# A relation layer in which POOL waits for free gather buffers once a step instead of once a unit

## The chip, the cores and the metric

The kernel runs on one core of a Trainium2 chip. The metric is the device time of one execution in microseconds (us). Engines are named as the profile names them: PE (TensorE matmul) and PEld (its weight loads), DVE (VectorE), ACT (ScalarE), POOL (GpSimd), SP (SyncE, which here only issues DMAs). "L796" is line 796 of the kernel.

## What is computed

A graph of N = 6250 nodes with 128 features and E = 200000 edges, sorted by destination. Two residual blocks, each followed by a layer norm: a two-layer weighted-mean aggregation, and then the relation layer that the change touches. Cut to that layer:

```python
# x1: the first block's result (6250, 128); 32 relations, 8 bases
hsrc = h[src]                                   # one row of x1 per edge
coef = w_comp[etype]                            # (E, 8)
msg = sum(hsrc @ weight[b] * coef[:, b][:, None] for b in range(8)) * norm
node_repr = segment_sum(msg, dst, num_segments=N) + bias_param
x = layernorm(x1 + relu(node_repr))
```

## The kernel before

The edges stand in 1568 tiles of 128. The first 428 tiles (REGION) are treated without gathers: their edges were sorted by source, and their source rows are made on PE by a product with a one-hot matrix (`sources`, L1283; ACT copies the result, L994; PE turns it, L1318; ACT copies that, L1001; "wide" products with it, L1326, which DVE adds up, L1777). The other 1140 tiles are gathered: POOL fetches one row of x1 for each of the 128 edges of a tile with an indirect DMA (L796).

The stage runs in 114 steps. A step has ten gathered tiles (STEP_TILES) in two units of five (UNIT_TILES), "tile 0" and "tile 1" of the step. A unit's five tiles are multiplied by PE (`tiles_summed`, L1309: ten matmul records, since each product is two in the trace) and the result is added into a ring of sums by DVE (`tile_added`, L1768). The gathered rows lie in G, which has room for HELD_UNITS = 7 units: unit n, where n = 2 x step + half, uses place n mod 7.

Each engine works through an order written out by hand, and semaphores tie them together. The counter s_u counts the units that PE has finished, in PE's order (`UNIT` gives a unit's number in it, with the wide and turned ones). s_gath[place] counts what has landed in a place; PE waits for it ahead of a unit's product (`tiles_summed`). The order of PE in a step s is: tile 0 of s (L1309), a part of the sources for step s+2 (L1283), two wide products (L1326), more sources, the finished blocks of nodes ("events", `block_multiplied`, L1345, which ACT takes in `block_taken`, L1020), two wide products, tile 1 of s (L1309), the last sources, the coefficients of s+2 (L1265, L1269), the turned sources of s+1 (L1318). Then tile 0 of s+1 follows. So tile 1 of a step and tile 0 of the next stand close together, and between tile 0 and tile 1 of one step lies most of its work. About every second step has an event.

DVE makes the one-hot matrices (L1718 to L1748), loads ring positions into registers (L1752) and adds. SP issues plain DMAs for the next steps.

POOL's program in this stage is only the loop that the change touches. Ahead of the first tile of each unit from the eighth on, it waits until PE has finished the unit that lies in the same place, seven units earlier. In the trace the wait is carried by the gather itself.

Of the kernel before, what the change touches and what calls it, by code (L numbers as in the profile page):

```python
# [38 lines left out]
HELD_UNITS = 7  # L39
# [195 lines left out]
def regular(nc, flag, x, src, dst, etype, w, w1, lin1, b1, lin2, b2, Wrel, wcomp, brel, out):  # L235
    with ExitStack() as ctx:
# [449 lines left out]
        def _(pool):  # L686
# [103 lines left out]
            for t in range(REGION, TILES):  # L790
                step, j = divmod(t - REGION, STEP_TILES)
                n, i = 2 * step + j // UNIT_TILES, j % UNIT_TILES
                if i == 0 and n >= HELD_UNITS:
                    half = n - HELD_UNITS
                    pool.wait_ge(s_u, UNIT[half // 2, "tile", half % 2] + 1)
                pool.indirect_dma_start(G[:, n % HELD_UNITS * UNIT_TILES + i, :], None, x1_d,  # L796
                                        bass.IndirectOffsetOnAxis(ap=SRC[:, t:t + 1], axis=0)).then_inc(s_gath[n % HELD_UNITS], 16)
# [2236 lines left out]
```

## Time and profile before

| | us |
|---|---|
| time, median of 3 runs (lowest to highest) | 3873.58 (3860.37 to 3875.08) |
| the profiled execution's own time | 3908.11 |
| its span, first to last instruction | 3906.3 |

The page's first two parts:

```profile
PE 3433.9 (88%) x17077; PEld 2289.0 (59%) x17077; DVE 2464.7 (63%) x4684; ACT 1351.4 (35%) x3452; POOL 2412.9 (62%) x2636
```

```profile
PE   3999999989989999999996888888888888888895
POOL 5888888870036675454523666666666666666662
PEclk6999999999999999999998888888888889888887
```

The first line is busy time, share of the span and number of instructions of each engine. In the strips the span is cut in 40 slices of 97.7 us, and a digit is the busy share in tenths; PEclk is the granted TensorE clock. The relation layer is the last 18 slices, from about 2100 us on. There PE is busy eight tenths of the time and POOL six, at a steady pace, and the clock is granted at 0.8 to 0.9.

### The profile page before, as it was taken

What the parts mean: (1) busy time and instruction counts of PE and PEld (TensorE: products, weight loads), DVE (VectorE), ACT (ScalarE), POOL (GpSimd) and SP (SyncE); (2) the same over time, 40 slices, a digit from 0 to 9 for tenths busy, and PEclk for the clock granted to TensorE, in tenths of its full rate; (3) what the DMA queues carried; (4) which work ended last, traced back from release to release, by engine and by line L of the source; (5) the groups of instructions that cost most, each with busy time, mean ns of one, the idle gap of its engine ahead of it and who ended that gap; (6) DMA issues with size and microseconds to landing.
All of it is one profiled execution on the core that took longest, in us unless ns stands there. A gap on an engine that the chain in (4) does not pass through costs nothing.

```text
span 3906.3 us, 52705 instructions
## 1 busy us (share of the span) xinstructions
PE 3433.9 (88%) x17077; PEld 2289.0 (59%) x17077; DVE 2464.7 (63%) x4684; ACT 1351.4 (35%) x3452; POOL 2412.9 (62%) x2636
## 2 busy tenths in 40 slices
PE   3999999989989999999996888888888888888895
PEld 3899999985533334444343555666555565555664
DVE  7999999986776663021032665666666666666674
ACT  5999999990000000010002222222222222222221
POOL 5888888870036675454523666666666666666662
PEclk6999999999999999999998888888888889888887
DMA  6677777778789999999993222222222222222221
GB/s 184 193 206 205 205 209 208 206 208 297 259 236 248 254 242 261 288 273 277 288 294 105 63 65 70 65 73 61 69 70 65 70 68 73 71 65 65 71 63 41
DMA packets 532789, 618.45 MB, mean 158 GB/s; under 512 B 74011, under 2 KB 460127, under 8 KB 532399
## 3 DMA queue, kind: packets, MB, share of 16 engines
q1 hardware_dynamic: 478895, 528.52, 47.3%
q0 software_dynamic: 53616, 86.51, 8.9%
q8 instruction: 140, 2.29, 0.2%
q14 instruction: 138, 1.13, 0.1%
HBM read 445.83 MB, written 168.99 MB: 157 GB/s over the span
## 4 chain that ended last, share of the span: by engine, by line
PE 47%; ACT 19%; DMA 9%; DVE 8%; issue 8%; another core or an unknown queue 7%; DVEq 2%; POOL 1%; SPq 0%; ACTq 0%; POOLq 0%
PE PS L1230 20%; ACT arena L844 11%; PE PS L1283 10%; DMA arena<-adjacency 8%; ACT arena L860 6%; PE PS L1309 5%; PE PS L1326 4%; PE PS L1269 2%; PE PS L1118 2%; DVE XT L1768 2%; PE PS L1345 1%; PE PS L1318 1%; DVEq L1752 1%; DVE H L1748 1%
## 5 line engine op out<-in xcount | busy, mean ns | idle before, releaser
L796 POOL DMA_INDIRECT arena<-x_table,rec x1140 | 1165.2, 1022 | 602.5 <-issue 311.0
L775 POOL DMA_INDIRECT sorted_records<-arena x428 | 494.2, 1155 | 590.4 <-PE PS L1230 495.3
L1118 PE MATMUL PS<-arena 128*98 128x128 f32 x6272 | 761.8, 279 | 46.6 <-DVE arena L1507 13.0
L1118 PEld LDWEIGHTS PS<-arena 128*98 128x98 f32 x6272 | 708.5, 166 | 96.4 <-issue 50.8
L732 POOL TENSOR_SCALAR arena<-iota,H,arena 128x98 f32<-128x98 f32 x980 | 677.5, 705 | 89.2 <-PE PS L1118 86.6
L1283 PE MATMUL PS<-H,X 128*128 128x512 bf16 x1568 | 549.3, 436 | 80.9 <-issue 76.4
L1230 PE MATMUL PS<-arena,X 128*128 128x512 f32 (+1 forms) x1274 | 543.8, 578 | 53.8 <-DMA arena<-adjacency 53.6
L844 ACT ACTIVATE arena<-arena 128x98 f32<-128x98 f32 x1568 | 583.4, 688 | 12.7 <-DVE arena L1505 12.7
L1230 PE MATMUL PS<-arena,H 128*128 128x512 f32 (+1 forms) x1274 | 531.9, 572 | 18.7 <-DMA arena<-adjacency 16.9
L1768 DVE TENSOR_TENSOR XT<-XT,PS 128x64 f32 x1140 | 252.5, 221 | 432.3 <-issue 198.4
L860 ACT ACTIVATE arena<-PS 98x1024 f32<-98x1024 f32 x392 | 520.5, 1328 | 12.6 <-PE PS L1118 12.6
L1686 DVE TENSOR_TENSOR arena<-arena 128x1536 f32<-128x1536 f32 (+1 forms) x192 | 344.1, 1792 | 174.0 <-DMA arena<-adjacency 168.1
L1507 DVE TENSOR_TENSOR arena<-PS,H 128x2048 f32<-128x2048 f32 x196 | 447.1, 2281 | 0.0
L1230 PEld LDWEIGHTS PS<-arena,X 128*128 128x128 f32 x1274 | 237.3, 192 | 339.1 <-issue 196.4
L1230 PEld LDWEIGHTS PS<-arena,H 128*128 128x128 f32 x1274 | 238.0, 190 | 300.8 <-issue 213.2
L1309 PE MATMUL PS<-arena 128*128 128x64 f32 x2280 | 325.3, 293 | 57.2 <-issue 45.8
L1309 PEld LDWEIGHTS PS<-arena 128*128 128x128 f32 x2280 | 323.0, 214 | 89.7 <-issue 55.8
L1283 PE MATMUL PS<-H,arena 128*128 128x512 bf16 x784 | 338.7, 432 | 6.2 <-issue 5.8
L1326 PE MATMUL PS<-arena 128*128 128x336 f32 x896 | 313.9, 474 | 27.9 <-issue 18.2
L1777 DVE TENSOR_TENSOR arena<-arena,PS 128x336 f32 x448 | 224.8, 502 | 178.1 <-remote 95.7
L1283 PEld LDWEIGHTS PS<-H,X 128*128 128x128 bf16 x1568 | 171.9, 116 | 266.2 <-issue 174.6
L994 ACT ACTIVATE rec<-PS 128x512 f32<-128x512 f32 x112 | 66.7, 596 | 677.7 <-remote 423.9
(259 smaller groups left out, 3148.0 us busy)
## 6 DMA issues: line engine op xcount, KB each, us to landing
arena<-adjacency SPq DMA_DIRECT2D x294, 768.0 KB
adjacency<-arena SPq DMA_DIRECT2D x196, 784.0 KB
arena<-adjacency SPq DMA_DIRECT2D x98, 832.0 KB
arena<-x_table,rec POOLq DMA_INDIRECT x1140
XT<-sorted_source_rows SPq DMA_DIRECT2D x112, 128.0 KB
arena<-in_edge_type SPq DMA_DIRECT2D x226, 48.0 KB
arena<-in_edge_type SPq DMA_DIRECT2D x226, 32.0 KB
XT<-sorted_relations SPq DMA_DIRECT2D x448, 8.0 KB
```

Source lines behind the costliest of these rows:

```text
L732: last = nc.gpsimd.tensor_scalar(S1[:, r, :], iota[:, 0:M1], K1T[:, v:v + 1], WWT[:, v:v + 1], ALU.is_equal, ALU.mult)
L775: pool.indirect_dma_start(rec2_d, bass.IndirectOffsetOnAxis(ap=SLOT[:, t:t + 1], axis=0), R4[:, t, :], None).then_inc(s_scat, 16)
L796: pool.indirect_dma_start(G[:, n % HELD_UNITS * UNIT_TILES + i, :], None, x1_d, bass.IndirectOffsetOnAxis(ap=SRC[:, t:t + 1], axis=0)).the ...
L844: nc.scalar.activation(S1[:, r, :], S1[:, r, :], ACT.Copy, scale=WWT[:, v:v + 1]).then_inc(s_wa, 1)
L860: nc.scalar.activation(ST[0:M1, n % 3, q * GROUP * P:(q + 1) * GROUP * P], PS[0:M1, q * GROUP * P:(q + 1) * GROUP * P], ACT.Copy).then_inc ...
L1118: last = nc.tensor.matmul(bank(2 * q + j // 4, P, j % 4 * P)[0:M1, :], S1[:, r, :], S2[:, r, :], start=True, stop=True)
L1230: last = nc.tensor.matmul(bank(bank0 + c, nb * P), (X, H1)[l][:, k, :], AB[n % 4][:, off:off + nb * P], start=(k == 0), stop=(k == NBLK - 1))
L1283: last = nc.tensor.matmul(bank(2), rows_part, ST2[i % 2][:, j, :], start=(j == 0 and a == 0), stop=(j == CLASS_BLOCKS - 1 and a == 2))
L1309: last = nc.tensor.matmul(bank(UNIT_BANKS[n % RING_BANKS], BASIS, j * BASIS), G[:, half % HELD_UNITS * UNIT_TILES + j, :], C[s % 2][:, fir ...
L1326: nc.tensor.matmul(bank(UNIT_BANKS[n % RING_BANKS], WIDE_BASIS), G2[i % 2][:, c, :], C2[i % 2][:, c, :, :].rearrange("p b j -> p (b j)"), ...
L1507: nc.vector.tensor_tensor(S2[:, whole, :], bank(4, P).unsqueeze(1).to_broadcast([P, BATCH, P]), each(K2T, n).to_broadcast([P, BATCH, P]), ...
L1686: nc.vector.tensor_tensor(ACC[p % 2][:, 0:width], ACC[p % 2][:, 0:width], AB[n % 4][:, 0:width], ALU.add).then_inc(s_acc, 1)
```

## The change

The one condition ahead of the gathers changes. Before, POOL waited at the first tile of each unit n (i == 0) for unit n - 7. After, it waits only at the first tile of a step (j == 0, n even), and for unit n + 1 - 7 = n - 6, the one whose place the second unit of this step will take. s_u counts in order, so unit n - 7 is then done as well. The ten gathers of a step follow without a further wait. The first wait comes at unit 6 instead of unit 7.

```diff
             for t in range(REGION, TILES):
                 step, j = divmod(t - REGION, STEP_TILES)
                 n, i = 2 * step + j // UNIT_TILES, j % UNIT_TILES
-                if i == 0 and n >= HELD_UNITS:
-                    half = n - HELD_UNITS
+                if j == 0 and n + 1 >= HELD_UNITS:
+                    half = n + 1 - HELD_UNITS
                     pool.wait_ge(s_u, UNIT[half // 2, "tile", half % 2] + 1)
                 pool.indirect_dma_start(G[:, n % HELD_UNITS * UNIT_TILES + i, :], None, x1_d,
```

## Rows read from the trace of the kernel before

**Rows 1.** The gathers' source line: count, ns min/median/max, who waited for it.

```profile
L796 POOL DMA_INDIRECT arena<-x_table,rec x1140: 941/947/2315, 2103.6 to 3848.2; - x190
...
who waited for it (us, times):
```

**Rows 2.** Timeline of PE, end of the stage: start, us, instruction.

```profile
3876.47 1.23 PE L1309 MATMUL PS<-arena 128*128 128x64 f32 x10
```

**Rows 3.** Windows view, whole stage: busy us of PE, PEld, DVE, ACT, POOL; clock, DMA.

```profile
2165.00:3848.20 1683.20, 1452.07 (x7461) 993.21 (x7458) 1084.99 (x3222) 438.07 (x1086) 1121.51 (x1097) 0.86 0.27 68
```

**Rows 4.** Waits of POOL, 2165 to 3850 us: us in total, times, longest.

```profile
POOL arena L796 <- issue: 298.8, 978, 0.7
POOL arena L796 <- PE PS L1309: 127.3, 47, 9.9
POOL arena L796 <- remote: 110.2, 55, 2.8
```

**Rows 5.** Timeline of POOL, first gathers of bursts, with idle before in brackets.

```profile
2151.92 0.94 POOL L796 DMA_INDIRECT arena<-x_table,rec  x1 [3.46 <-remote]
...
3083.08 1.46 POOL L796 DMA_INDIRECT arena<-x_table,rec  x1 [1.93 <-PE PS L1309]
...
3112.78 0.96 POOL L796 DMA_INDIRECT arena<-x_table,rec  x1 [2.27 <-PE PS L1309]
...
3143.02 1.10 POOL L796 DMA_INDIRECT arena<-x_table,rec  x1 [2.01 <-PE PS L1309]
...
3203.41 0.94 POOL L796 DMA_INDIRECT arena<-x_table,rec  x1 [2.19 <-remote]
3218.06 0.95 POOL L796 DMA_INDIRECT arena<-x_table,rec  x1 [2.15 <-remote]
```

**Rows 6.** Timeline of PE, 3068 to 3220 us: unit products and one event.

```profile
3112.18 0.30 PE L1309 MATMUL PS<-arena 128*128 128x64 f32 x1 [0.51 <-issue]
...
3115.54 1.23 PE L1309 MATMUL PS<-arena 128*128 128x64 f32 x10
...
3141.53 1.22 PE L1309 MATMUL PS<-arena 128*128 128x64 f32 x10
...
3145.38 1.23 PE L1309 MATMUL PS<-arena 128*128 128x64 f32 x10
...
3195.59 1.95 PE L1345 MATMUL PS<-XT,Wr 128*128 128x128 f32 x16
```

**Rows 7.** Timeline of ACT, the event's copy.

```profile
3202.98 0.37 ACT L1020 ACTIVATE H<-PS,bcol 128x128 f32<-128x128 f32 x1 [11.64 <-remote]
```

**Rows 8.** Windows view, sums: first 8 us of nine bursts; then rest up to next.

```profile
sum 72.00, PE 70.86 PEld 46.73 DVE 41.74 ACT 32.51 POOL 56.63; mean PE 7.87 PEld 5.19 DVE 4.64 ACT 3.61 POOL 6.29
...
sum 63.00, PE 45.93 PEld 33.39 DVE 44.39 ACT 2.42 POOL 35.38; mean PE 5.10 PEld 3.71 DVE 4.93 ACT 0.27 POOL 3.93
```

**Rows 9.** Windows view of PE, eight steps: length, PE busy, clock, DMA.

```profile
3082.30:3095.80 13.50, 12.18 (x61) 0.87 0.32 69
3095.80:3116.80 21.00, 16.16 (x82) 0.84 0.24 60
3116.80:3134.20 17.40, 15.14 (x62) 0.72 0.23 58
3134.20:3146.60 12.40, 12.40 (x63) 0.84 0.16 42
3146.60:3163.80 17.20, 14.71 (x79) 0.85 0.45 108
3163.80:3175.10 11.30, 11.30 (x63) 0.93 0.28 66
3175.10:3190.00 14.90, 12.00 (x62) 0.86 0.27 71
3190.00:3206.30 16.30, 13.83 (x78) 0.92 0.26 65
```

**Rows 10.** Timeline of all engines, 2928 to 2932 us: a long gather beside DVE.

```profile
2928.56 1.56 DVE L1740 TENSOR_TENSOR arena<-XT 128x1344 f32<-128x1344 f32 x1
2928.84 2.10 POOL L796 DMA_INDIRECT arena<-x_table,rec  x1 [0.30 <-issue]
```

## Prediction, written before the change was run

> **What bounds the kernel now.** I read the views in this order: the gathers' own source line, the waits of POOL, the stage's window, and then the timelines of POOL, PE and ACT side by side over nine steps. The first view says who cares about the gathers: the 1140 of them take 0.947 us in the median, and under "who waited for it" nothing stands [rows 1]. The ring of seven buffers keeps POOL far ahead: the last gather starts at 3848.2 us, and PE multiplies the last unit at 3876.47 us, 28 us later [rows 1, 2]. So no engine waits for a row of x1, and a delay of some microseconds in the gathers delays nobody by their data.
>
> That would end the case at "no change", if POOL's busy time did nothing else. But the stage shows two more things.
>
> First, POOL has little time to spare. From 2165.0 to 3848.2 us it is busy 1121.5 us with 1097 gathers, 1.022 us each on average [rows 3], and between two gathers of a unit there are 0.30 us (298.8 us in 978 pieces [rows 4]). Ten gathers are 10 x (1.022 + 0.30) = 13.2 us. Nine bursts of ten in a row start at 3083.08 and end with the start at 3218.06 [rows 5], so one burst with its pause lasts 134.98/9 = 15.0 us. The stage as a whole takes 1683.2 us/1097 x 10 = 15.3 us for ten gathers. PE's mean step is the same by construction: PE, DVE and POOL all turn at 15 us.
>
> Second, the pauses of POOL are strange, and they are not POOL's alone. In the nine bursts each pause is about 2 us, also where the buffer had long been free. And what others wait for seems to arrive at that same moment. PE ends an event's product (L1345) at 3195.59 + 1.95 = 3197.54 us [rows 6]; ACT, idle since 3191, takes it only at 3202.98 us and the trace names no engine that released it ("remote") [rows 7]; POOL starts its next burst at 3203.41 us after a pause of 2.19 us [rows 5]. So in the later part of a burst a blocked engine is woken late, together with POOL, when the burst has drained. Over nine bursts, PE is busy 70.86 of the 72.00 us that are the first 8 us of each, and 45.93 of the 63.00 us from there to the next burst; ACT 32.51 us against 2.42 us [rows 8]. PE thus loses (63.00 - 45.93)/9 = 1.9 us per burst, nearly all in its last part. I take this as the stage's real limit: PE's work is broken up by the bursts. The why isn't in the trace. The Trainium skill, "DMA: Bandwidth & Descriptors", section "Anatomy of one DMA — SWDGE (gpsimd) path", gives a DMA issued from GpSimd about 2.0 us of fixed time, most of it until its last write is confirmed; that is an estimate of 2.2 us for the 64 KB of one gather, and would fit a pause that ends when the last gather has landed, though no row here has a landing for the gathers.
>
> **The change, part by part.** A unit is five gathers; unit 2s and unit 2s+1 belong to step s.
> Removed: the wait ahead of the odd unit 2s+1, for the first product (L1309) of step s-3. Its instructions: the gaps inside a burst of ten are 0.30 us whether or not a wait stands there, since nine bursts of ten hold nine such waits without a pause. So nothing is won: 0 us.
> Moved: that same wait now stands ahead of the even unit 2s, in place of the wait for the second product of step s-4. The first product of step s-3 comes later than the second of step s-4: the two end at 3142.75 and 3146.61 us, at 3.9 us distance, in a step where POOL went on at 3143.02, 0.27 us after the first of them; in the step before, they ended at 3112.48 and 3116.77 us and POOL had gone on at 3112.78 [rows 5, 6]. With PE's times as they are, POOL would start at 3117.04 and 3146.88, 4.3 and 3.9 us later. Behind the wait stand only the gathers (POOL does nothing else, and no plain DMA is in its queue in this stage), and for them nobody waits: the lead of 28 us or more covers 4 us. By data the cost is 0; without that cover it would be 3.9 us a step.
> What a later burst does to the others is not shown directly, so I bound it. Eight steps of PE, cut where each step's first product ends, take 13.5, 21.0, 17.4, 12.4, 17.2, 11.3, 14.9 and 16.3 us, 124.0 us together [rows 9]. Now POOL may be up to 3.9 us late or early against PE without holding it: the long steps of 21.0 and 17.4 us are followed by one of 12.4 us, and POOL goes on in its 15.0 us. After the change each burst also waits until the step's first product has ended, so a long step shifts the grid of bursts, and a step shorter than 15.0 us can't win it back as far as PE needs a wake-up that comes when the burst is drained.
> Upper bound: no step is won back. Each step takes the longer of 15.0 us and its own time: 15 + 21.0 + 17.4 + 15 + 17.2 + 15 + 15 + 16.3 = 131.9 us, +7.9 us in eight steps, +0.99 us a step, +110 us in the 111 steps behind the first three.
> Lower bound: the long steps are long only because of the bursts, and the new alignment takes that away. Then each takes the longer of 15.0 us and its busy time (16.2, 15.1, and below 15 [rows 9]): 121.3 us, -2.7 us in eight steps, -0.34 us a step, -37 us.
> Neither row is nearer; I take the middle, +36 us.
> The start: with seven buffers free POOL gathers 35 in a row and pauses 3.46 us, until 2151.92 us [rows 5]. After the change it stops after 30, since unit 6 now asks for unit 0's buffer; 5 x 1.25 us = 6 us earlier the waiting engines are woken: -6 us.
> Sum: 36 - 6 = +30 us.
>
> A rule that bears on where the gathers fall: a gather that starts at 2928.84 us takes 2.10 us while DVE runs a 1.56 us product (L1740) from 2928.56 us [rows 10]; the median is 0.947 us. The Trainium skill, "SBUF — State Buffer", the box in its section "SBUF: two separate sides", says that DVE work in a two-port mode locks GpSimd out of the port pair it needs to write its descriptors. By that rule moved bursts meet other DVE work. The number of long gathers would change, but both kernels run the same DVE instructions each step, so the sum stays.
>
> **Rivals.**
> A. Nothing that can be measured. For it: nobody waits for a gather [rows 1], and the wait only moves by 3.9 us under a cover of 28 us. The loss of PE in late bursts (1.9 us a burst) then stays what it is, and only the start differs: 3874 - 6 = 3868 us. It would hold if the late wake-ups depend on the number of gathers alone.
> B. Faster. The bursts become regular, and start at a point where PE has just finished a product, so that PE has most of a step before the bad part. For it: in step 3163.8 to 3175.1 PE needs only 11.3 us with no idle [rows 9]. By the lower bound 3874 - 37 - 6 = 3831 us; as the middle of this case 3850 us.
> C. Slower, the forecast: the wait for the later product takes the slack between POOL and PE away, and late steps are no longer won back. It decides from the point where PE's step is over 15.0 us, which it is in 4 of 8 steps [rows 9]. 3874 + 30 = 3904 us, at most 3874 + 110 - 6 = 3978 us.
> D. The change doesn't do what it says: POOL pauses after five gathers still. Speaks against it: in these nine bursts it doesn't even now, and the wait in the middle is gone. It would give the time of A.
>
> **How the numbers follow.** The profiled execution took 3908.11 us (span 3906.3), 34.5 us or 0.9% more than the median of the three times, 3873.58 us (3860.37 to 3875.08). The sum is made against 3908.11 us, so a profile of the changed kernel should have about 3938 us; a difference carries over, and the median becomes 3873.6 + 30 = 3904 us. About 0.5% (19 us) is what a measurement can tell from no change. Chances: C 0.5 (of which 0.04 lies under the 19 us), A and D 0.27, B 0.23 (0.02 of it within 19 us). Faster by over 0.5%: 0.21; within: 0.33; slower: 0.46. The likeliest case alone reaches from 3880 to 3950 us. The range for all is 3842 to 3950 us: below it lies the far half of B, above it the upper third of the way to the rigid bound.
>
> **What would show it.** In the profile after: bursts of ten and never five, starting 0.3 us behind the end of a step's first L1309 product or later; still nobody under "who waited for it" of the gathers; POOL's waits for PE L1309 up from 127 us [rows 4]. For C: PE idle in the stage up, with steps rarely under 15 us. For A: the same PE idle per burst, though the starts have moved. For B: PE's steps of 11 to 13 us become more frequent. The forecast is wrong if late wake-ups follow something other than the bursts, for then moving a burst moves nothing; and its size is wrong if POOL is so far behind PE that the new wait is mostly met on arrival.

## The result and the profile after

| | before | after |
|---|---|---|
| median of 4 runs (lowest to highest), us | 3871.73 (3860.37 to 3875.08) | 3987.16 (3971.56 to 4003.59) |
| the profiled execution, us | 3908.11 | 3989.01 |

The changed kernel is slower: ratio 1.029, interval 1.0262 to 1.0317, or 115 us. The direction was forecast, the size was not: 3904 us was predicted and the range ended at 3950.

The first two parts of the page of after, to be laid beside those of before (busy us, share and instructions of each engine; then busy tenths in 40 slices, now of 99.7 us):

```profile
PE 3483.4 (87%) x17077; PEld 2315.0 (58%) x17077; DVE 2480.7 (62%) x4684; ACT 1342.4 (34%) x3452; POOL 2426.4 (61%) x2636
...
PE   3999999989999999999977888888878888887886
...
POOL 6888888860056774555316666666656656656663
PEclk6999999999999999999987888888888888878887
```

The numbers of instructions are the same, so nothing was added. The loss lies in the relation layer. Its gathers in after, by their source line (the view of [rows 1]: ns min/median/max, first and last start; then POOL's idle time ahead of them by what ended it):

```profile
L796 POOL DMA_INDIRECT arena<-x_table,rec x1140: 938/945/2107, 2072.3 to 3933.9; - x190
...
  PE PS L1309: 322.0, 75
  issue: 313.3, 1028
  remote: 58.5, 35
...
who waited for it (us, times):
```

From the first to the last gather it took 1744.6 us before and takes 1861.6 us now: +117 us, close to the 115 us between the medians. (The profiled execution of before was one that reached this stage 31 us later than that of after; that is why the two profiled times are only 81 us apart.) A gather lasts as long as it did, and still nobody waits for one.

The stage in the windows view, the one row that answers [rows 3] (busy us of PE, PEld, DVE, ACT, POOL with instructions; clock, DMA share, GB/s):

```profile
2165.00:3933.90 1768.90, 1476.64 (x7337) 996.54 (x7336) 1078.10 (x3159) 420.52 (x1065) 1101.93 (x1075) 0.84 0.25 63
```

For ten gathers, about a step, that is 1768.90/1075 x 10 = 16.45 us, of which PE is busy 13.74 and idle 2.72. Before it was 1683.20/1097 x 10 = 15.34 us, busy 13.24 and idle 2.11. Of the +1.1 us a step, 0.6 us is idle PE and 0.5 us is PE busy longer with the same matmuls; the granted clock, 0.84 against 0.86, accounts for some 0.3 of it (13.24 x 0.86/0.84 = 13.56).

Who waits in that stage (the view of [rows 4], all engines, 2165 to 3960 us; us in total, times, longest; "remote" means that the trace names no instruction and no DMA as the releaser):

```profile
ACT rec L994 <- remote: 740.4, 76, 13.9
ACT H L1020 <- remote: 326.0, 30, 13.7
POOL arena L796 <- PE PS L1309: 320.3, 74, 12.6
...
POOL arena L796 <- issue: 295.3, 969, 0.3
...
PE PS L1283 <- issue: 112.7, 68, 4.8
...
PE PS L1265 <- ACT H L1020: 65.5, 19, 5.8
...
POOL arena L796 <- remote: 51.7, 33, 2.4
```

POOL's waits for the product rose from 127.3 us in 47 cases [rows 4] to 320.3 in 74, while its "remote" ones fell from 110.2 to 51.7. ACT's copy L994 was ended by "remote" 44 times for 423.9 us in the same view of before, and now 76 times for 740.4 us. (These are whole idle times, not lateness: on a chip where nothing comes late, ACT still waits 588.8 us ahead of L994, as shown further down.) PE's wait at L1265 for ACT's event copies rose from 12.7 us in 10 cases to 65.5 in 19.

One long step shows how these hang together. From the timelines of after, all engines merged in time (start, duration, instruction, idle before it):

```profile
2173.49 0.67 PE L1309 MATMUL PS<-arena 128*128 128x64 f32 x5 [1.22 <-issue]
2174.43 0.94 POOL L796 DMA_INDIRECT arena<-x_table,rec  x1 [2.93 <-PE PS L1309]
...
2180.45 1.95 PE L1345 MATMUL PS<-XT,Wr 128*128 128x128 f32 x16
...
2185.78 1.16 POOL L796 DMA_INDIRECT arena<-x_table,rec  x1 [0.30 <-issue]
2188.68 0.28 ACT L1008 ACTIVATE XT<-PS 128x128 f32<-128x128 f32 x1 [11.66 <-remote]
...
2189.10 0.61 PE L1265 MATMUL PS<-wcd,XT 128*128 128x32 f32 x2 [3.22 <-ACT XT L1008]
...
2191.94 2.23 PE L1309 MATMUL PS<-arena 128*128 128x64 f32 x10
2194.44 0.94 POOL L796 DMA_INDIRECT arena<-x_table,rec  x1 [7.50 <-PE PS L1309]
...
2209.16 0.94 POOL L796 DMA_INDIRECT arena<-x_table,rec  x1 [1.11 <-remote]
```

The first product of the step ends at 2174.16 us and POOL starts its ten gathers 0.27 us later. PE ends the event's product at 2182.40. ACT has been idle since 2177.02 and takes it only at 2188.68, 6.3 us later and 1.7 us after the last gather's end at 2186.94. PE then waits for ACT (3.22 us), its next first product ends at 2194.17, and POOL, whose own gathers have long landed, has waited 7.50 us for it. That burst took 20.0 us, the next 14.7.

The trace holds two more things about that delay. The DMA packets of the gathers are recorded, though no landing is matched to an instruction: the last packet of this burst ends at 2188.22 us, 1.3 us behind the last gather's end (1.24 us in the median of all bursts of after, 1.26 before) and 0.46 us before ACT starts. And the event product's semaphore update is itself recorded at 2188.66 us, 0.02 us ahead of ACT's start, as in the median of both traces. So the trace doesn't tell a signal that comes late from a sleeper that is woken late; "late wake-up" here means no more than the delay.

Counted over the whole trace (my own grouping of the records; bursts are split where POOL pauses over 0.7 us; a step runs from the end of one first product to the next; events are those from the first gather to 15 us behind the last burst's start):

| | before | after |
|---|---|---|
| bursts in the stage | 35, then 25 of five, 80 of ten, 12 of fifteen | 30, then 111 of ten |
| bursts of ten: followed within 15.5 us, mean | 65, 14.92 us | 76, 14.86 us |
| bursts of ten: followed later, mean | 15, 17.50 us | 34, 19.92 us |
| 43 steps with an event, mean | 17.63 us | 19.90 us |
| 67 steps without, mean | 13.76 us | 14.09 us |
| from the end of the event's product to ACT's copy, mean of 47 | 3.6 us | 5.0 us |
| event's product ends 6 to 8 us into a burst | 9 | 20 |
| source products (L1283) that ended while ACT waited for them, from 2165 us on | 84 | 72 |
| of these, ended in the first 4 us of a burst: number, longest delay | 30, 0.04 us | none |
| of these, ended 6 to 12 us into a burst | 34 | 68 |
| from the end of the source product to ACT's copy L994, sum of all of these | 181 us | 287 us |

So of 119 us in 110 steps, 43 x 2.27 = 97 us lie in the steps that have an event. Now that a burst follows the first product of its step, the event's product ends 6 to 8 us into the burst in 20 of 47 cases (9 of 47 before), where its reader is woken 5.7 us late on average. The source products show it still more plainly: in before a copy whose product ended in the first 4 us of a burst was never late, and after the change no source product ends there while ACT waits; 68 of 72 end 6 to 12 us into the burst, and ACT takes each of these over 0.5 us late, 4.2 us on average. How much of that reaches PE isn't told by the count; the steps without an event grew by 0.33 us.

### The profile page after: what moved, and what is told of

Its sections match the earlier page's. It is cut to its first block, busy times and chain, and to the rows that moved or that the text cites. A ratio compares the mean times of both kernels' runs of the same rounds, so it can differ in the third digit from the quotient of the medians.

```text
span 3987.2 us, 52705 instructions
## 1 busy us (share of the span) xinstructions
PE 3483.4 (87%) x17077; PEld 2315.0 (58%) x17077; DVE 2480.7 (62%) x4684; ACT 1342.4 (34%) x3452; POOL 2426.4 (61%) x2636
## 4 chain that ended last, share of the span: by engine, by line
PE 47%; ACT 20%; another core or an unknown queue 16%; DMA 7%; issue 6%; DVE 3%; POOL 1%; DVEq 0%; SPq 0%; ACTq 0%; POOLq 0%
PE PS L1230 21%; ACT arena L844 11%; PE PS L1283 9%; DMA arena<-adjacency 6%; ACT arena L860 5%; PE PS L1309 5%; PE PS L1326 4%; PE PS L1269 2%; PE PS L1118 2%; PE PS L1318 2%; PE PS L1345 1%; PE PS L1265 1%; PE PS L1162 0%; PE PS L1163 0%
## 5 line engine op out<-in xcount | busy, mean ns | idle before, releaser
L775 POOL DMA_INDIRECT sorted_records<-arena x428 | 506.8, 1184 | 546.5 <-PE PS L1230 450.0
L1283 PE MATMUL PS<-H,X 128*128 128x512 bf16 x1568 | 578.6, 457 | 129.9 <-issue 129.7
L844 ACT ACTIVATE arena<-arena 128x98 f32<-128x98 f32 x1568 | 584.0, 689 | 12.7 <-DVE arena L1505 12.6
L1309 PE MATMUL PS<-arena 128*128 128x64 f32 x2280 | 326.4, 289 | 54.2 <-issue 53.9
L1283 PEld LDWEIGHTS PS<-H,X 128*128 128x128 bf16 x1568 | 173.3, 118 | 337.2 <-issue 262.2
L1309 PEld LDWEIGHTS PS<-arena 128*128 128x128 f32 x2280 | 322.5, 211 | 77.9 <-issue 56.8
L1283 PE MATMUL PS<-H,arena 128*128 128x512 bf16 x784 | 357.4, 456 | 0.1
L994 ACT ACTIVATE rec<-PS 128x512 f32<-128x512 f32 x112 | 66.6, 595 | 810.6 <-remote 770.4
L1326 PE MATMUL PS<-arena 128*128 128x336 f32 x896 | 324.4, 489 | 12.6 <-issue 12.3
```

What stands on the lines that cost most here:

```text
L775: pool.indirect_dma_start(rec2_d, bass.IndirectOffsetOnAxis(ap=SLOT[:, t:t + 1], axis=0), R4[:, t, :], None).then_inc(s_scat, 16)
L844: nc.scalar.activation(S1[:, r, :], S1[:, r, :], ACT.Copy, scale=WWT[:, v:v + 1]).then_inc(s_wa, 1)
L1283: last = nc.tensor.matmul(bank(2), rows_part, ST2[i % 2][:, j, :], start=(j == 0 and a == 0), stop=(j == CLASS_BLOCKS - 1 and a == 2))
L1309: last = nc.tensor.matmul(bank(UNIT_BANKS[n % RING_BANKS], BASIS, j * BASIS), G[:, half % HELD_UNITS * UNIT_TILES + j, :], C[s % 2][:, fir ...
L1326: nc.tensor.matmul(bank(UNIT_BANKS[n % RING_BANKS], WIDE_BASIS), G2[i % 2][:, c, :], C2[i % 2][:, c, :, :].rearrange("p b j -> p (b j)"), ...
```

## The experiments

The theory: bursts of gathers keep sleeping engines from being woken; the change locks the burst to the step, so that the products that others wait for end where the wake-up is latest. It splits in two: (a) the missing stop between the units, which gave sleepers a second chance in a step, and (b) the later product that the burst waits for. The rival: the bursts are innocent and the loss is PE's or the clock's own. The runs went to seven other chips, which I call A to G. The kernel before stood beside every run; ratios are to it on the same chip.

**Chip A: each part alone, and thin gathers.** The ring is given an eighth place in free words of the arena. The changed kernel with eight places waits once a step, for unit n - 7 as before: part (a) alone. (G_at takes the place of G's slice where a tile is gathered and where it is multiplied.)

```diff
-HELD_UNITS = 7
+HELD_UNITS = 8
...
-        G = cut(0, HELD * D).rearrange("p (t c) -> p t c", c=D)
+        G_at = lambda t: cut(t * D, D) if t < 35 else cut(5760 + (t - 35) * D, D) if t < 39 else cut(13568, D)
...
-                if i == 0 and n >= HELD_UNITS:
-                    half = n - HELD_UNITS
+                if j == 0 and n + 1 >= HELD_UNITS:
+                    half = n + 1 - HELD_UNITS
```

> The changed kernel with an eighth buffer (HELD_UNITS = 8): still one wait a step and ten gathers in a row, but the wait is now for unit n - 7, the second product of step s-4, the same product that the kernel before waits for at its even units. Lost slack (the later product is what costs): the loss of 113 us goes, 3860 to 3885 us. Ten in a row (the missing stop in the middle is what costs): it stays near 3985 us. The same PE idle per burst as before (1.9 us) for the first, 2.7 us for the second.

The same eight places with before's wait for each unit (the diff without its last four lines):

> The kernel before with the eighth buffer and its waits per unit, now for unit n - 8: the even unit waits for the first product of step s-4, nearly a whole step earlier than before. Lost slack: with more slack between POOL and PE than before, faster or the same as before, 3830 to 3875 us. Ten in a row: as before, 3872 us.

Before's wait for each unit with six places, so that the even unit waits for the product that the change makes it wait for, and the stop in the middle stays: part (b) without (a).

```diff
-HELD_UNITS = 7
+HELD_UNITS = 6
```

> The kernel before with six buffers instead of seven and its waits per unit: the even unit waits for unit n - 6, the very product that the changed kernel waits for, and the odd unit waits for the second product of the same step. Lost slack: as slow as the changed kernel or slower, 3975 to 4040 us. Ten in a row: bursts are broken in the middle, so about as before, 3870 to 3900 us.

Only the first tile of each unit is gathered, and PE multiplies it in place of all five (the matmul's own line of the diff is left out here):

```diff
+                if i:
+                    continue
                 pool.indirect_dma_start(G[:, n % HELD_UNITS * UNIT_TILES + i, :], None, x1_d,
...
-                pe.wait_ge(s_gath[half % HELD_UNITS], 16 * rows_until(half))
+                pe.wait_ge(s_gath[half % HELD_UNITS], 16 * rows_until(half) // UNIT_TILES)
```

> The kernel before, but POOL gathers only the first tile of each unit, 228 gathers instead of 1140, and PE uses that tile for all five products (so the gathered messages are not the reference's). All products, additions and waits stay. If the bursts of gathers hold up PE by late wake-ups: PE's idle time in the stage falls from about 220 us to under 60 us, ACT's waits without a named releaser (424 us at L994 alone) nearly vanish, and the stage is 100 to 250 us shorter. If PE's idle time has nothing to do with the gathers: within 20 us of before.

Measured, beside 3769.52 us for before (27 runs): after8 3768.39 us, ratio 1.000 (0.9986 to 1.0013); before8 3773.81, 1.0013 (0.9999 to 1.0026); before6 3770.39, 1.0002 (0.9986 to 1.0018); thin 3748.34, 0.9946 (0.9925 to 0.9968). The differences that were expected of the two eights and the six rested on late wake-ups, and this chip shows none (an event is taken 0.04 us behind its product in the median): the kernel before itself takes 102 us less than on the first. (In the relation layer itself the gap is larger, some 160 us for before: from first to last gather the kernels with six, seven and eight places take 1575 to 1600 us on chips A, B, D, E and F, against 1744.6 on the first; the first chip reached this layer 20 to 60 us earlier than A, B, D and E.) So nothing follows for the parts; the first question became whether the change costs anything here at all.

**Chip B: the change itself, and before's profile.** The changed kernel as it is:

> The changed kernel itself, beside the kernel before on the same chip. The chip of the four experiments before this one showed no late wake-ups: bursts of up to 500 gathers without a pause, no waits without a releaser, and 3770 us for the kernel before instead of 3872 us. If late wake-ups are what makes the changed kernel slow, it is no slower than before where the chip shows none (within 0.3%), and about 2.9% slower where it does. If the new wait costs by itself (PE or POOL waiting longer), it is slower on every chip by about 113 us.

The kernel before as it is, for its profile:

> The kernel before, for its profile on this chip. Late wake-ups as a property of the chip or its condition: no pause of POOL without a wait for PE, PE idle in the stage under 120 us instead of 219 us, nothing at L994 under remote if the chip is like the last one; if it is like the first one, the rows of before again.

The changed kernel with a wait for a still later product, unit n - 5:

```diff
-                if j == 0 and n + 1 >= HELD_UNITS:
-                    half = n + 1 - HELD_UNITS
+                if j == 0 and n + 2 >= HELD_UNITS:
+                    half = n + 2 - HELD_UNITS
```

> The changed kernel with its one wait a step moved further, to the second product of step s-3 (unit n - 5, about 8 us later still). Late wake-ups present, lost slack: no slack was left to lose, so as slow as the changed kernel or more, 3980 to 4060 us. Late wake-ups absent: as before within 0.5%, since two and a half steps of lead still cover it.

Before, with POOL also waiting ahead of each unit until its own last one has landed:

```diff
+                if i == 0 and n:
+                    pool.wait_ge(s_gath[(n - 1) % HELD_UNITS], 16 * rows_until(n - 1))
```

> The kernel before, with one more wait of POOL ahead of each unit: for the landing of its own previous unit (s_gath), so that every burst is five gathers and drains before the next. Where the chip shows late wake-ups: blocked engines are woken every 8 us, PE idle falls to about 0.4 us per five gathers, but POOL's step becomes 2 x 8 = 16 us, so the stage is bound by POOL at 114 x 16 = 1824 us, 40 to 100 us slower than before. Where it shows none: POOL still has 16 us a step against PE's 14 us, so PE now waits for gathers and the kernel is about 114 x (16 - 14) = 230 us slower than before there.

Measured, beside 3769.20 us for before (19 runs): after 3769.05 us, ratio 0.9995 (0.9982 to 1.0009); late 3770.46, 0.9992 (0.9979 to 1.0005); pause 4052.60, 1.0732 (1.07 to 1.0764). The profiled execution of before took 3778.32 us. Its trace tells why the change is free here. Waits of before on chip B from 2165 to 3740 us, and its window:

```profile
ACT rec L994 <- PE PS L1283: 588.8, 109, 11.9
...
ACT H L1020 <- PE PS L1345: 235.7, 31, 10.2
...
POOL arena L796 <- PE PS L1309: 75.1, 39, 4.9
```

```profile
2200.00:3700.00 1500.00, 1342.06 (x7201) 904.52 (x7200) 1050.43 (x3112) 433.31 (x1050) 1109.38 (x1075) 0.91 0.30 75
```

No wait here is ended by "remote": ACT is released by the product that it waits for (0.04 us behind the event's product in the median). A step takes 1500/1075 x 10 = 13.95 us, not 15.34, and the clock is granted at 0.91, though the DMA engines move more here (75 GB/s against 68 [rows 3]). The changed kernel on chip B has the same picture, with the gathers following one another straight away 1102 times of 1140:

```profile
L796 POOL DMA_INDIRECT arena<-x_table,rec x1140: 938/944/2292, 2125.5 to 3710.7; - x190
...
  issue: 335.9, 1102
  PE PS L1309: 71.8, 29
```

The pauses made POOL the bound. Waits of that kernel and the starts of its bursts (its lines are two further down):

```profile
POOL arena L798 <- DMA arena<-x_table,rec: 391.5, 204, 4.0
...
PE PS L1311 <- DMA arena<-x_table,rec: 333.5, 121, 5.4
```

```profile
2610.33 0.94 POOL L798 DMA_INDIRECT arena<-x_table,rec  x1 [1.85 <-DMA arena<-x_table,rec]
...
2618.16 1.03 POOL L798 DMA_INDIRECT arena<-x_table,rec  x1 [1.89 <-DMA arena<-x_table,rec]
```

Here the landing itself is in the trace: 1.85 us behind the last gather's end, and five gathers with their pause take 7.8 us in this place. Over the stage (first gather at 2140.2, last at 4029.8 us) a unit takes 1889.6/228 = 8.3 us, against 1586.5/228 = 7.0 us in before on chip B; that is the loss. It is 283 us, where about 230 were expected: a unit takes 8.3 us and not the 8 that the estimate had. PE's clock is granted at 0.85 in this stage (2200 to 3900 us), without any late wake-up. The Trainium skill, "DMA: Bandwidth & Descriptors", section "Anatomy of one DMA — SWDGE (gpsimd) path", puts the fixed part of a DMA issued from GpSimd, set-up and completion together, at about 2.0 us. The trace is near that if it is counted from the end of the gather's instruction, 1.85 and 1.89 us; from its start it is 2.8 us. It also fits the pauses of about 2 us on the first chip [rows 5]: there the last packet of a burst ends 1.26 us behind its last gather (median) and POOL goes on 0.7 us later, without having asked for that.

**Chip C: a chip with late wake-ups.** The kernel before takes 3951.26 us here (3 runs). The two kernels are those of chip A with eight places and one wait a step, and with thin gathers.

> The kernel of e1_after8 again, in the hope of a chip that shows late wake-ups, as the one of before and after did (kernel before near 3872 us; the two chips since then: 3770 us). If it does: lost slack gives 3860 to 3885 us, ten in a row gives 3985 us. If it doesn't: as the kernel before, 3770 us.

> The kernel of e4_thin again (one gather of five, the rest of the work kept), beside e9_after8. On a chip with late wake-ups: the whole difference between the chips comes from POOL's bursts, so it falls to the 3748 us that it has on the chips without. If the chip is slower for another reason: it stays about 100 us above 3748 us.

Measured: the thin kernel 3752.90 us, ratio 0.950 (0.9473 to 0.9528). That is within 5 us of what it takes on chip A, where before is 182 us faster, and the two agree to 0.2 us from first to last gather (1551.0 and 1551.2 us). Its waits and window (lines two further down):

```profile
POOL arena L798 <- PE PS L1311: 1265.1, 214, 13.3
ACT rec L996 <- PE PS L1285: 531.3, 99, 12.0
ACT H L1022 <- PE PS L1347: 229.1, 31, 10.4
```

```profile
2200.00:3700.00 1500.00, 1340.55 (x7181) 919.75 (x7295) 1039.67 (x3146) 436.24 (x1057) 225.60 (x212) 0.91 0.15 37
```

"remote" is gone, ACT takes an event 0.04 us behind its product in the median, and the clock is back at 0.91. So the whole difference between such a chip and the others is made by the gathers, lower clock included, and the rival falls. (Of the 198 us that thinning saves here, 21 us are saved on chip A too, where nobody is woken late.) Whether it is their unbroken rows or their bytes isn't split by this kernel, which takes away four fifths of both.

After8 took 4041.52 (the profiled execution) and 3976.62 us, 1.023 and 1.006 times before: +90 and +25 us, neither the time of before that "lost slack" gives nor clearly the whole loss of "ten in a row". With two executions 1.6% apart, the cost of part (a) alone isn't measured; no interval can be given. What its profile shows of the mechanism:

```profile
ACT rec L994 <- remote: 342.6, 32, 31.9
...
POOL arena L796 <- PE PS L1309: 269.9, 51, 14.0
```

```profile
2365.96 0.95 POOL L796 DMA_INDIRECT arena<-x_table,rec  x1 [2.47 <-PE PS L1309]
...
2405.59 0.94 POOL L796 DMA_INDIRECT arena<-x_table,rec  x1 [12.48 <-PE PS L1309]
```

With eight places POOL sometimes runs through two steps. Between these two starts lies one burst of twenty gathers, and it cost 39.6 us for two steps. Twelve such bursts stand in the trace, with about 12 us of PE idle in each on average. In its other bursts the place isn't fixed as in after: of 96 source products that ended while ACT waited, 49 ended in the first 4 us of a burst and were taken at once, and ACT's delays at L994 sum to 156 us, not 287.

**Chips D, E and F: looking for another chip of that kind.** The changed kernel, before with six places, after with eight, and before, on chip D:

> The changed kernel again. On a chip with late wake-ups: 2 to 4% slower than the kernel before. On one without: within 0.3% of it.

> The later product alone, with the stop in the middle kept (six buffers, waits per unit; the even unit waits for the product that the changed kernel waits for). With late wake-ups: lost slack gives the same loss as the changed kernel, 2 to 4%; the missing stop gives a result within 1% of the kernel before, or a faster one, since bursts of five are then more frequent. Without late wake-ups: within 0.3%.

> The missing stop alone (eight buffers, one wait a step, for the product that the kernel before waits for at its even units). With late wake-ups: lost slack gives the time of the kernel before; the missing stop gives most of the changed kernel's loss. Without: within 0.3%.

> The kernel before, for its profile on this chip. With late wake-ups: PE idle over 150 us in the stage and waits of ACT at L994 without a releaser of several hundred us. Without: the rows of e8_before.

On chip E:

> The changed kernel again. On a chip with late wake-ups: 2 to 4% slower than the kernel before. On one without: within 0.3% of it.

> The later product with the stop in the middle kept (six buffers, waits per unit). With late wake-ups: lost slack gives the loss of the changed kernel; the missing stop gives the time of the kernel before or less. Without: within 0.3% of the kernel before.

On chip F:

> The later product with the stop in the middle kept (six buffers, waits per unit), a last look for a chip with late wake-ups (two of six so far). There, lost slack gives 2 to 4% over the kernel before, the missing stop gives the time of the kernel before or less. Without late wake-ups: within 0.3% of it.

Measured: chip D, before 3772.67 us (25 runs): after 3770.36 us, 0.9992 (0.998 to 1.0004); before6 3772.39, 1.0003 (0.9989 to 1.0017); after8 3772.06, 0.9994 (0.9977 to 1.0012); the profiled execution of before 3768.40. Chip E, before 3772.06 (17 runs): after 3776.03, 1.0015 (0.9999 to 1.0031); before6 3770.03, 0.9989 (0.9974 to 1.0004). Chip F, before 3706.04 (13 runs): before6 3708.04, 1.0003 (0.9991 to 1.0015). None of the three shows late wake-ups. These runs can't split the cost, but they settle that without late wake-ups nothing in this family moves the time: three chips with the changed kernel, four with six places, two with eight.

**Chip G: late wake-ups again,** before 3950.39 us (11 runs).

> As e17_before6: with late wake-ups, lost slack gives 2 to 4% over the kernel before, the missing stop gives the time of the kernel before or less; without, within 0.3% of it.

Measured: 3941.54 us, ratio 0.9989 (0.9968 to 1.0009), no difference. Waits from 2165 to 3870 us:

```profile
ACT rec L994 <- remote: 393.1, 43, 15.8
...
POOL arena L796 <- PE PS L1309: 133.6, 45, 9.3
POOL arena L796 <- remote: 123.0, 60, 3.0
```

These are close to the numbers of before on the first chip (423.9 us in 44 cases; 127.3 in 47 and 110.2 in 55 [rows 4]). Behind the first 30 gathers its bursts are 31 of five, 85 of ten and 7 of fifteen, and ACT takes an event 3.6 us late on average; 41 of 92 source products end in the first 4 us of a burst. So on this chip a ring that makes even units wait for the later product costs nothing as long as POOL may stop between the units, as the missing stop would have it and lost slack would not.

## Why the prediction was right in direction and wrong in size

**Nobody waits for a gather: held.** The list is empty in both [rows 1]. The last unit's gathers start at 3933.9 us, and its product comes 25 us later.

**A burst of ten with its pause is 15.0 us: held.** 76 of 110 bursts of after follow one another in 14.86 us.

**Late wake-ups are the limit: held, and shown by the thin kernel on chip C,** where 198 us go with the gathers and 21 us on a chip without late wake-ups. What I didn't consider is that they might belong to the chip. The prediction argued from one chip's trace as if from the kernel; on five of eight chips its forecast C has no ground at all, and A (no difference) is what was measured on three of them.

**The removed wait at 0 us: this step failed.** I reasoned that nine bursts of ten contain nine such waits without a pause [rows 5]. That holds for the nine, but they were a chosen stretch: in the whole stage POOL stopped at the odd unit often enough to make 25 bursts of five and 12 of fifteen. "Remote" waits of the other engines end 7.2 us after the start of a burst of five (median of 10) and 14.5 us after that of one of ten (107), and PE's idle time grows faster than the burst: in before it is 0.3 to 0.5 us in a burst of five, 1.9 in one of ten and 5.3 to 5.5 in one of fifteen, by where a burst is cut off from the next. What the runs show in place of the 0 us: with the stop kept, the later product costs nothing (chip G, 0.9989); with the stop gone as well, the two cost 115 us (first chip); with the stop gone alone, two executions lie 25 and 90 us over before (chip C). That a wait usually costs nothing on its own engine said nothing about what its pause gave the others.

**The moved wait at +36 us: the mechanism put into it was half right.** Chip G says that the later product alone takes nothing away (+36 expected by this step, measured -9 us by the medians, -13 to +4 by the interval of the ratio). What costs, as the traces have it, is the fixed place of the burst in the step, which takes both parts: of the four traces with late wake-ups, only in after do the awaited source products never end in a burst's first 4 us. I had a rigid grid in mind in which every step lasts at least 15.0 us; but 33 of 110 steps of after are still shorter than 14.5 us (56 before). Most of the loss came from the other end, in steps with an event, at 19.9 us against 17.6. The upper bound, +0.99 us a step, lies close to the +1.08 us measured, but that is luck: it left PE's busy time as it was, while nearly half of the loss is matmuls that last longer, and it took the loss from short steps. I took the middle between bounds for want of a nearer row. There was one: in the example of [rows 6, 7] an event's reader is woken 5.4 us late, and setting the ends of the dependent products against the step's first product was the thing to do: after the change 20 of 47 events end 6 to 8 us into a burst, and 68 of 72 source products 6 to 12 us.

**The start at -6 us: held for the burst.** From the first gather to the second burst it was 48.3 us (2103.6 to 2151.92 [rows 1, 5]) and is now 42.7 us (2072.3 to 2115.03). That the time fell by it isn't shown.

**Rivals.** A fell on the first chip, and its time, that of before, is what B, D and E show; its reason, wake-ups that depend on the number of gathers alone, isn't tested there, since none are late. B fell: the bursts did become regular, and that was the harm. D fell: 111 bursts of exactly ten. Of the signs named, "bursts of ten, starts behind the first product" (63 of 107 within 1 us of it), "waits for L1309 up" and "PE idle up" came; "steps rarely under 15 us" didn't.

**What stays open.** The two parts were never measured with the change itself on chip C or G, so how the 115 us divide between the missing stop and the burst's new place isn't settled; part (a) alone has two runs 1.6% apart. The 115 us themselves come from one chip, four executions each. That the alignment of the products with the burst carries the loss is read from step lengths and delays in the traces, and no run moved the products alone. Bursts broken by force, gathers whole, were run only where nobody is woken late, so rows and bytes aren't told apart. Why some chips wake engines late isn't in any trace here. No version that gathers every tile beat both kernels: where nobody is woken late, six and eight places and the later wait are equal to before, and forced pauses lost 7.3%.

## What to carry to other kernels

That nobody waits for an engine's data doesn't make the timing of its DMAs free: ask which other engines are asleep while it issues a row of them, and when they are woken. A wait that looks idle can be the pause in which they are, so before removing one, count the pauses over the whole stage and set the ends of the dependent products against the phase of the burst. Where a trace shows "remote" wake-ups, take a second chip's trace before believing a few per cent either way.

## What the runs showed of the hardware

Eight chips ran the kernel before, in 3706 us (F), 3769 to 3773 us (A, B, D, E), 3872 us (the first), and 3950 and 3951 us (G, C). Chip F's lead isn't in the relation layer: in the traces taken there and on A, B, D and E, it gets there after 2058 us, the others after 2124 to 2140 us, and with six places it takes 1591 us from first to last gather, against 1588 to 1592 us there. On the first chip, C and G, an engine that waits is mostly released in the later part of an unbroken row of indirect DMAs only about when the row has landed, 1.7 us behind the last gather's end in the step shown; of the late releases by an event on the first chip, 37 of 40 before and 30 of 42 after came behind the row's last gather, the rest in the middle of a row. On the other five ACT takes an event within 0.04 us in the median. The price rises faster than the row's length: about 0.1, 0.2 and 0.4 us of idle PE per gather in rows of five, ten and fifteen on the first chip, and 0.6 in rows of twenty on chip C. And PE's granted clock is lower where PE is more idle in this stage: 0.91 where nobody is woken late (chip B, and the thin kernel on chip C), 0.86 and 0.84 on the first chip before and after, and 0.85 on chip B with forced pauses, where PE waits for gathers.
